# Two attention layers on one Trainium2 core: in the second layer the heads weigh the context itself instead of values made from it

## The reference, cut to what matters

```python
def _cross_attention(q_in, kv_in, wq, bq, wk, bk, wv, bv, wo, bo, bias_k, bias_v):
    qh = (q_in @ wq + bq).reshape(b, q_len, H, K)
    kh = (kv_in @ wk + bk).reshape(b, t, H, K)
    vh = (kv_in @ wv + bv).reshape(b, t, H, K)
    kh = jnp.concatenate([kh, jnp.broadcast_to(bias_k, (b, 1, H, K))], axis=1)
    vh = jnp.concatenate([vh, jnp.broadcast_to(bias_v, (b, 1, H, K))], axis=1)
    scale = jnp.sqrt(jnp.asarray(K, q_in.dtype))
    logits = jnp.einsum('bqhk,bthk->bhqt', qh, kh) / scale
    weights = jax.nn.softmax(logits, axis=-1)
    ctx = jnp.einsum('bhqt,bthk->bqhk', weights, vh).reshape(b, q_len, H * K)
    return ctx @ wo + bo
```

## Time and profile before

| | |
|---|---|
| time, median of 3 runs | 2775.32 us (2772.16 to 2776.03) |
| profiled execution, span | 2770.6 us |
| PE busy | 2534.8 us, 91% |
| PEld, DVE, ACT, POOL busy | 80%, 55%, 39%, 26% |
| HBM read, written | 118.14 MB, 11.08 MB |
| DMA queue q1 (SP), q10 (ScalarE) | 107.37 MB, 12.67 MB |

### The profile page before, as it was taken

One profiled execution on the slowest core, in us unless ns is written; L12 is line 12 of the kernel. 1 busy time (PEld: TensorE's weight loads), 2 busy tenths in 40 slices (PEclk: granted clock), 3 DMA queues, 4 the chain that ended last, 5 costly groups with the idle time before them and its releaser, 6 DMA issues. The chain is left out here.

```text
span 2770.6 us, 47590 instructions
## 1 busy us (share of the span) xinstructions
PE 2534.8 (91%) x14224; PEld 2214.7 (80%) x14224; DVE 1526.2 (55%) x3532; ACT 1068.2 (39%) x2657; POOL 709.3 (26%) x730
## 2 busy tenths in 40 slices
PE   5988599999979999998978885999999799999988
PEld 4766498988969898897856664989989698898967
DVE  3777645455454545455457766454554545455455
ACT  3777133333323333332237762333333233333322
POOL 2012404223030413302721033132140313223035
PEclk8999799999989999998989997999999899999989
DMA  5001202011010201102330021011020201111033
GB/s 182 8 15 34 81 9 61 23 38 45 15 49 15 61 15 45 38 0 80 96 98 16 8 67 55 16 46 34 26 61 8 56 10 50 30 30 38 0 98 84
DMA packets 74022, 120.67 MB, mean 44 GB/s; under 512 B 6481, under 2 KB 27985, under 8 KB 73969
## 3 DMA queue, kind: packets, MB, share of 16 engines
q1 hardware_dynamic: 66416, 107.37, 13.8%
q10 hardware_dynamic: 7552, 12.67, 1.6%
HBM read 118.14 MB, written 11.08 MB: 47 GB/s over the span
## 5 line engine op out<-in xcount | busy, mean ns | idle before, releaser
L420 PE MATMUL pj<-ctx_hi,wk_hi 128*128 128x376 f32 x1160 | 396.8, 342 | 0.0
L421 PE MATMUL pj<-ctx_lo,wk_hi 128*128 128x376 f32 x1160 | 391.3, 337 | 0.0
L422 PE MATMUL pj<-ctx_hi,wk_lo 128*128 128x376 f32 x1160 | 390.5, 337 | 0.0
L362 POOL TENSOR_SCALAR wk_hi<-raw 128x512 fp32r<-128x512 f32 x74 | 45.9, 620 | 1330.8 <-ACTq L951 921.9
L1048 DVE SCALAR_TENSOR_TENSOR k_lo<-pj,cur,k_hi 128x375 fp32r<-128x375 f32 x256 | 155.4, 607 | 320.5 <-ACT k_hi L777 320.5
L420 PE MATMUL pj<-wv_hi,ctx_hi 128*125 128x512 f32 x768 | 305.6, 398 | 0.0
L421 PE MATMUL pj<-wv_lo,ctx_hi 128*125 128x512 f32 x768 | 302.5, 394 | 0.0
L422 PE MATMUL pj<-wv_hi,ctx_lo 128*125 128x512 f32 x768 | 302.3, 394 | 0.0
L777 ACT ACTIVATE k_hi<-pj,cur 128x375 fp32r<-128x375 f32 (+1 forms) x274 | 157.3, 574 | 375.4 <-PE pj L422 375.4
L425 PEld LDWEIGHTS tp<-ident,probs 112*125 112x125 f32 (+1 forms) x1536 | 200.0, 165 | 86.2 <-DVE wk_lo L1046 32.8
L425 PE MATMUL tp<-ident,probs 112*125 112x112 f32 (+1 forms) x1536 | 231.3, 273 | 25.6 <-DVE pt_lo L1046 12.4
(11 more groups left out here) (145 smaller groups left out, 5835.7 us busy)
## 6 DMA issues: line engine op xcount, KB each, us to landing
raw<-in_wq SPq DMA_DIRECT2D x74, 256.0 KB, 3.0
raw<-in_wk SPq DMA_DIRECT2D x74, 256.0 KB, 3.0
raw<-in_wo SPq DMA_DIRECT2D x72, 256.0 KB, 2.6
raw<-in_wv SPq DMA_DIRECT2D x64, 256.0 KB, 3.0
raw<-in_w SPq DMA_DIRECT2D x64, 256.0 KB, 2.9
ctx_copy<-in_ctx_t SPq DMA_DIRECT2D x2, 3000.0 KB, 13.2
ctx_lo<-ctx_copy SPq DMA_DIRECT2D x8, 750.0 KB, 8.7
ctx_copy<-in_ctx_t ACTq DMA_DIRECT2D x4, 750.0 KB, 8.7
```

The lines of the kernel that those rows point to most:

```text
L362: nc.gpsimd.tensor_scalar(hi, src, 1.0, 0.0, ALU.mult, ALU.add).then_inc(split_hi, 1)
L420: nc.tensor.matmul(dst, l_hi, r_hi, start=first, stop=False)
L421: nc.tensor.matmul(dst, l_hi, r_lo, start=False, stop=False)
L422: return nc.tensor.matmul(dst, l_lo, r_hi, start=False, stop=last)
```

## The change

The product P (ctx Wv) is taken as (P ctx) Wv. For a group of four heads, R = P ctx is made per batch and chunk of 128 context columns, for the four heads at once (448 columns), and then R Wv per pair of batches and head (224 columns). The row of bias_v less bv goes in as one small matmul per unit with 12 rows (`bx` by `ex`); `ex` is gathered from the split weights of the softmax by small DMAs. The context in natural order (375 rows on partitions, as 3 x 125; hi and lo together are KC = 125 rows of NAT = 3072 values) is made once per batch by transposes on TensorE, split into hi and lo in a staging buffer, stored to DRAM and loaded again for every group and batch into one buffer `nat`. The values' buffers are gone; wq and wv share one buffer "b". The loops over halves, attentions and MLP pieces are unrolled; the loop over groups stays on the computing engines and is unrolled on SP and GpSimd. In the opening the context comes straight from the input. `natural` is three units of four 128x125 transposes for a batch; in the MLP it stands behind the four `out_part` of a piece. `values1` is 12 matmuls of 224 columns and then `bx` by `ex`.

```diff
-    ctx_dram = nc.dram_tensor("ctx_copy", (D, B, S), F32, kind="Internal").ap()
+    ctx_dram = nc.dram_tensor("ctx_copy", (D, HB, S), F32, kind="Internal").ap()
+    nat_dram = nc.dram_tensor("nat_scratch", (B, KC, NAT), F32, kind="Internal").ap()
+        nat = sb("nat", [P, NAT], F32R)
-        w_hi = {n: sb(f"w{n}_hi", [P, DC, GW], F32R) for n in "qkvo"}
+        w_hi = {n: sb(f"w{n}_hi", [P, DC, GW], F32R) for n in "bko"}
@@ SP @@
+                def store_nat(half, b, freed):
+                    sp.wait_ge(pj_free, freed + PJ)
+                    sp.dma_start(nat_dram[half * HB + b], stage[half][b % 2][0:KC, :].bitcast(F32)).then_inc(nat_out[b % 2], 16)
...
+                def load_nat(b):
+                    sp.dma_start(nat[0:KC, :].bitcast(F32), nat_dram[hf * HB + b]).then_inc(nat_in, 16)
...
+                if hf == 0:
+                    for b in range(HB):
+                        store_nat(0, b, at["pre"] + PRE[0]["n", b, SC - 1] + 1)
+                    sp.dma_start(ctx_dram, ctx_t[:, HB:B, :]).then_inc(ctx_copied, 16)
...
+                for ag in range(NG):
...
+                    load_rows(base + RAW_A + ag * RAW_GU + 2 * DC, wo, ag * GW, 0)
+                    load_rows(base + RAW_A + ag * RAW_GU + 3 * DC, wv, a * D, g * GW)
+                    for b in range(2):
+                        store_extra(b)
+                        sp.wait_ge(pj_ready, gpj + GU["r", b, DC - 1] + 1)
+                        sp.sem_inc(sp_passed, 1)
+                        load_nat(b + 1)
+                    sp.wait_ge(pj_ready, gpj + GU["v", 0, HPG - 1] + 1)
+                    store_extra(2)
+                    if ag + 1 < NG:
+                        load_k(ag + 1)
+                    sp.wait_ge(pj_ready, gpj + GU["r", 2, DC - 1] + 1)
+                    sp.sem_inc(sp_passed, 1)
+                    load_nat(3)
+                    store_extra(3)
+                    if ag + 1 < NG:
+                        sp.wait_ge(pj_ready, gpj + GU["r", 3, DC - 1] + 1)
+                        sp.sem_inc(sp_passed, 1)
+                        load_nat(0)
+                        load_q(ag + 1)
...
+                for m in range(MLPG):
...
+                    load_rows(mb, w1, 0, m * GW)
+                    if m > 0 and hf == 0:
+                        store_nat(1, m - 1, at["mlp"] + m * padded(MLP_U[0]))
+                    load_rows(mb + DC, w2, m * GW, 0)
@@ PE @@
+            def natural(half, b, base, k=1):
...
+                    def weigh1(b, c):
...
+                        if c == 0:
+                            pe.wait_ge(nat_in, (ag * HB + b + 1) * 16)
+                            pe.wait_ge(tp_free, gtp + b * HPG + HPG + TP)
+                        pe.wait_ge(pj_free, gpj + unit + 1)
+                        for s in range(SC):
+                            last = three(pj[unit % PJ][:, 0:T],
+                                         [n[0:KC, s, c * P:(c + 1) * P] for n in nat_parts],
+                                         [p[0:KC, :, s * L:(s + 1) * L] for p in pt_parts], s == 0, s == SC - 1)
...
+                    def values1(pair, h):
...
+                            three(dst, [w["b"][:, c, h * P:(h + 1) * P] for w in (w_hi, w_lo)],
+                                  [r[:, c, h, :] for r in r_parts], c == 0, False)
...
+                    q_stage(gpj, use_b)
+                    for b in range(HB):
+                        keys1(b, 0)
+                        if b == 1:
+                            scores1(0, 3)
+                        keys1(b, 1)
+                        if b > 0:
+                            transpose1(b - 1, 0)
+                            transpose1(b - 1, 1)
+                        keys1(b, 2)
+                        scores1(b, 0)
+                        if b == HB - 1:
+                            for h in range(HPG):
+                                values1(0, h)
+                        if b > 0:
+                            transpose1(b - 1, 2)
+                            transpose1(b - 1, 3)
+                        keys1(b, 3)
+                        scores1(b, 1)
+                        if b > 0:
+                            weigh1(b - 1, 0)
+                        scores1(b, 2)
+                        if b > 0:
+                            weigh1(b - 1, 1)
+                            scores1(b, 3)
+                            weigh1(b - 1, 2)
+                            weigh1(b - 1, 3)
+                    for h in range(HPG):
+                        transpose1(HB - 1, h)
+                    out1(0)
+                    for c in range(DC):
+                        weigh1(HB - 1, c)
+                    out1(1)
+                    for h in range(HPG):
+                        values1(1, h)
+                    out1(2)
+                    out1(3)
...
+                for m in range(MLPG):
...
+                    if hf == 0:
+                        natural(1, m, mpj + HPG + HB, 1 + MLP_PAD[0])
@@ ScalarE @@
+            def natural(half, b, base):
+                if b > 1:
+                    act.wait_ge(nat_out[b % 2], (half * HB // 2 + b // 2) * 16)
...
+                for n in nat_out:
+                    act.wait_ge(n, (hf + 1) * HB // 2 * 16)
...
+                        if pair == 1 and h == HPG - 1:
+                            act.sem_inc(w_free["b"], 1)
```

More of the change, by code:

```diff
@@ new lines, in padded, with pre_units, pre_mids @@
+def padded(n):
+    return -(-n // PJ) * PJ
+def pre_units(half):
+    names = [("n", 0, s) for s in range(SC) if half == 0] + [("vt", 0)]
+    for b in range(HB):
+        if b + 1 < HB:
+            names += [("n", b + 1, s) for s in range(SC) if half == 0] + [("vt", b + 1)]
+        names.append(("v", b))
+    return names
+def pre_mids(half):
+    names = [("n", 0, s) for s in range(SC) if half == 0] + [("vt", 0)]
+    for b in range(HB):
+        names += [("n", b + 1, s) for s in range(SC) if half == 0 and b + 1 < HB] + [("v", b)]
+        names += [("vt", b + 1)] if b + 1 < HB else []
+    return names
@@ new lines, in xattn_program @@
+        r_parts = [rr[:, i * RH:(i + 1) * RH].rearrange("p (c h n) -> p c h n", c=DC, h=HPG) for i in range(2)]
+        pt_parts = (pt_hi, pt_lo)
+        nat_parts = [nat[:, i * SC * D:(i + 1) * SC * D].rearrange("p (s n) -> p s n", s=SC) for i in range(2)]
+        ot0 = [rr[:, i * C0 * T:(i + 1) * C0 * T].rearrange("p (c t) -> p c t", c=C0) for i in range(2)]
+        place_sel = rr[:, 2 * C0 * T:2 * C0 * T + 2 * HPC * P].rearrange("p (e j m) -> p e j m", e=2, j=HPC)
+        at_q0 = 2 * C0 * T + 2 * HPC * P
@@ new lines, in _ @@
+                for c in range(C1):
+                    load(base + RAW_C + 2 * c, wq0[:, c * P:(c + 1) * P].rearrange("(c p) n -> p c n", p=P), (DC, P))
+                    load(base + RAW_C + 2 * c + 1, wk0[:, c * P:(c + 1) * P].rearrange("(c p) n -> p c n", p=P), (DC, P))
+                load_rows(base + RAW_W0, wo0, 0, 0)
+                load_k(0)
+                load_q(0)
+                sp.wait_ge(v0c_ready, (hf + 1) * C0 * 2)
+                for n in nat_out:
+                    sp.wait_ge(n, (hf + 1) * HB // 2 * 16)
@@ L352, in _, with split_free @@
                 pool.sem_inc(s, 1)
-            def split(half_base, n, shape, hi, lo, signal, k):
+            def split_free(n, shape, hi, lo, signal, k, done):
                 slot = n % 2
@@ new lines, in weights, with columns0 @@
+            def weights(n, name, free, use):
+                pool.wait_ge(w_free[name], free + 1)
+                for c in range(DC):
+                    split_free(n + c, (1, GW), w_hi[name][:, c, :], w_lo[name][:, c, :], w_ready[name], 1,
+                               use * DC + c + 1)
+            def columns0(n, name, parts, pieces, free, use):
+                pool.wait_ge(w_free[name], free + 1)
+                k = DC // pieces
+                for i in range(pieces):
+                    hi, lo = (f[:, k * P * i:k * P * (i + 1)].rearrange("p (c n) -> p c n", n=P) for f in parts)
+                    split_free(n + i, (k, P), hi, lo, w_ready[name], k, use * DC + k * (i + 1))
@@ L472, in values_t @@
                     if b == 0:
-                        pe.wait_ge(w_ready["v"], hf * WV_H * DC + DC)
+                        pe.wait_ge(w_ready["b"], hf * WB_H * DC + DC)
                     for c in range(DC):
-                        last = three(pj[unit % PJ][:, 0:SK], [f[:, c * P:(c + 1) * P] for f in flat["v"]],
+                        last = three(pj[unit % PJ][:, 0:SK], [f[:, c * P:(c + 1) * P] for f in wv0_parts],
                                      (ctx_hi[:, c, b, :], ctx_lo[:, c, b, :]), c == 0, c == DC - 1)
@@ L501, in queries0 @@
                         pe.wait_ge(pj_free, base + unit + 1)
-                        pe.wait_ge(w_ready["q"], use * DC + DC)
+                        pe.wait_ge(w_ready["b"], use * DC + DC)
                     for c in chunks:
```

(14 more changed lines are left out.)

1124 lines of the change are left out of this document (573 added, 551 removed).

## The result

The changed kernel takes 3232.45 us (median of four runs, 3226.37 to 3244.41) beside 2774.27 of the kernel before (2772.16 to 2776.03): ratio 1.166, 95% interval 1.163 to 1.168. It is slower by 458 us, where 362 were forecast. The profiled execution has a span of 3228.4 us, 457.8 more than before.

What follows compares the result with a forecast made beforehand. The group was taken as pure TensorE, so any wait costs its whole length 16 times. Groups 260, opening 36, MLP 60 and second opening 6 gave +362 on 2770.6 plus 4.7: 3137, said as 3140, range 2980 to 3340.

Steps and rivals of the forecast that it cites:

- the three waits: Per group on PE: 3.8 us before batch 1's R, 8.8 before batch 3's, 9.1 before q in 12 of 16 groups.
- its own signs: Load 13 to 17 us, 130 packets; PE idle 12 us for nat, 9 before q_stage; clock under 0.9; period 133 us.
- The load of the natural context on five engines: Loading `nat` per batch: 125 rows share equally over 5 engines at most, so 14.3 us, 14.5 with the signal.
- Rival 1: Loading `nat`: all 16 engines share it, 6.3 us, total 2742 and faster; chance 12%.
- rivals 2 and 3: Loading `nat`: 10 us, total 2870, chance 6%; or one engine, 72 us, total over 5000, chance 3%.
- The waits for nat: PE before R in each group: batch 1 waits 3.8 us, batch 3 8.8, batches 2 and 0 none.
- The q weights: Next group's wq loads stand behind batch 0's context load: first head 9.1 us late in 12 of 16 groups, 6.8 on average.
- The clock: After each long PE gap in a group, half-clock matmuls lose 1.5 us; 4.1 us per group.
- The dense work: Group's TensorE work: values and weighing, 49.3 us, go; R, 29.1, and R Wv, 11.5, come; net -8.7 us.
- transposes' stall: Batch 3's four softmax transposes stand together on two `tp` banks and stall 1.45 us per group.
- The product form alone (rival 4): Groups with every load hidden and nothing waiting: -139 us, total 2636; chance 1%.
- Openings and MLP: Outside the groups: opening +36 us, MLP of the first half +60, second opening +6.

Runs made afterwards that it cites:

- e1: Changed kernel with each natural-context load as two DMAs, rows 0 to 111 and 112 to 124: 2989.1 us, 1.078 of the kernel before.
- e11: Changed kernel with each natural-context load as one DMA of 128 rows instead of 125: 2916.1 us, 1.051 of the kernel before.
- e3: Changed kernel with the next group's four wq loads issued ahead of batch 0's natural-context load: 3159.1 us, one run.
- e7: Changed kernel with idle matmuls added, 16 ahead of batch 1's first R and 48 ahead of batch 3's: 3173.9 us, 1.144 of the kernel before.
- e4: Changed kernel without the context reloads, R computed from whatever stands in the buffer, for pricing only: 2868.2 us, 1.035 of the kernel before.
- e12: Changed kernel with 128-row ScalarE loads, split stores, 128-row `bx`, transposes split, `out1(1)`, w2, wq0, wk0 earlier, copy later: 2736.1 us, 0.987 of before.
- e8: Changed kernel with loads and stores split, loads from ScalarE, 128-row `bx`, batch 3's transposes split, w2 earlier: 2867.0 us, 1.033 of before.

## Why the prediction was right, and where it fell short

It had the cause right, five engines for 125 rows, and the three waits that come of it; it fell short by 96 us of 458. Of its own signs, the packets and the load's time came as named. The clock of a group (0.91, under 0.9 named), the wait for nat (14.1, about 12 named) and the group's period (142.0, 133 named) missed by little, and the idle time before q_stage was 5.4 and not 9, since part of that stall is slow matmuls.

**The load of the natural context on five engines: right.** Forecast 130 packets and 14.3 us, 14.5 with the signal. The trace has 130 packets, a share of 5 in 16 and, from issue to use, 13.9 us for batch 1 and 15.4 for batch 3. The Trainium skill's rule (DMA: Bandwidth & Descriptors, section Why a DMA increments its semaphore by 16 and not by 1) is that the count is the largest up to 16 that divides the slowest dimension: 5 for 125, 16 for 112 and 128, 13 for 13. The small packets of e1 and e11, 29 and 16, agree. The recorded estimate of 5.5 us goes by a fit that stands in the same page's section Anatomy of one DMA, and not in its section Bandwidth, and is given there for DMAs issued from GpSimd; for these loads of 125 rows the trace has 13.9 and 15.4 us. Rival 1 (2742, all engines share) and rivals 2 and 3 are out by the same rows.

**The waits for nat: right in kind, 1.5 short.** Forecast 3.8 and 8.8, measured 3.6 and 10.5. The step said that batch 3's load is issued when the last R of batch 2 is done. But SP was busy with four wk loads from 586.48 to 594.8, and issued `nat` behind them at 594.93, 1.0 us after the last R (593.56 + 0.37), where batch 1's load followed its R after 0.1. That is 0.9 of the 1.7 by which batch 3's wait was short; I had named this queue for the q weights and not here. The load itself is another 0.9: 15.4 us, beside the tail of those wk loads, in place of 14.5.

**The q weights: right.** Forecast the first chunk usable 15.3 after the last R, the head done after 25.7, 9.1 late; measured 15.9, 26.7, and 8.6 late. e3 took most of it away and gave 73 us, 6.1 for each of twelve groups; a wait of 2.0 us stays.

**The clock: right in kind, its size a little off.** For the two gaps before R 3.0 us were forecast (1.5 each); filling them gave back 4.0 (e7), and the table below leaves 3.4. The third gap, before the q head, was priced at 9.1 of waiting and 1.5 of clock; measured, the two together are the 8.6 above, 3.2 of them slow matmuls.

**The dense work: this failed.** "R Wv, 8 units x 13 = 104 matmuls of 224 columns ... I take 0.11: 11.5 us": the 0.11 is right for twelve of thirteen. The thirteenth contracts 12 rows, and I priced it by its columns alone. All 104 took 14.4 us. R took 29.8 for 29.1, and about 1.3 lie in the rest. The group from 505.4 to 646.3, term by term:

| term | forecast | measured |
|---|---|---|
| dense work at full clock | 108.3 | 113.2 (e4's group less its waits) |
| transposes' stall | 1.45 | 1.6 |
| waits for nat | 12.6 | 14.1 |
| delay of the first q head | 9.1 | 8.6 |
| other half clock | 4.5 | 3.4 (what is left) |
| sum | 136.0 | 140.9 |

So of about 6 us per group by which the forecast fell short (361 less 260, by 16), some 3 are the 12-row matmul, 2 other dense work, and 1.5 the waits for `nat`, in about equal parts the queue ahead of batch 3's load and the load's own length.

**The product form alone (rival 4): too good.** It was said to bring 139 us if nothing waited. e4, where nothing waits for a load, has a group of 117.6 beside 117.2: of the 8.7 us saved per group 4.9 were never there, and the transposes and the split of q take back the rest. The change's arithmetic gain was nearly nothing even before its loads. With 128 rows and the transposes split (e12) it is 3 us per group.

**Openings and MLP: right in sum** within 5 us each: 31, 65 and 15 for 36, 66 and 16, and the first query matmul at 82.4 for 81 to 83. In the MLP of the first half that is partly luck:

```profile
1519.10:1664.80 145.70, 109.52 (x423) 84.49 (x424) 41.06 (x67) 21.86 (x30) 45.63 (x48) 0.80 0.21 72
```

It takes 145.7 us in place of 87.3, 58 more for a forecast of 60. But PE idles 36.2 of them, where the waits for VectorE and w2 were put at 51, and it is busy 22.3 longer, where the transposes and the clock were put at 9: at a clock of 0.80 in place of 0.97 the slow matmuls took what the waits did not.

## What to carry to other kernels

Look at the number of rows of a large transfer before its bytes: 125 rows ran on 5 engines, 128 rows with the same data and three rows of filling on 16, in half the time (7.3 us in place of 15.4 for batch 3). Price a matmul by how many rows it contracts as well as by its columns, and keep a short contraction out of a chain of full ones or pad it with zeros. When a load has a fixed window between its last reader and its next, count everything that the queue and the engines do in that window, and test improvements together, since part of a removed cost is waited for at the next place (e8: 122 us of 201).

## What was not expected of the hardware

A matmul of 12 rows between matmuls of 128 cost 0.38 us more than its columns. The Trainium skill (TensorE: Matmul & The Clock Gate, section Why this matters for your kernels) has a single matmul of 32 rows at the same time as one of 128. Here 12 rows within a chain of 128-row matmuls were not so, and for such a chain the measurement decides.

Two DMAs of 112 and 13 rows had the engines busy for a share of 0.80 and moved 210 GB/s over the whole load (e1); one DMA of 128 rows moved 277 at a share of 0.74 (e11). By the packets 112 rows are 7 to an engine and 128 are 8, so why a row takes 0.75 us in the pair and 0.54 in the single DMA stays open.

Idle matmuls in two waits of 3.6 and 10.5 us per group made the kernel 59 us faster, though they do none of its work (e7).
